# Attention one: the last pair's shift goes behind all scores, the scores are reordered, and the maximum's mask becomes one 128-row product a bank

## The reference

```python
def _L0_attn_ref(x, Wqkv, bqkv, Wr, br):
    xh = x.reshape(b, c, h, he).transpose(0, 2, 1, 3)
    qkv = jnp.einsum('bhce,ef->bhcf', xh, Wqkv) + bqkv
    q, k, v = jnp.split(qkv, 3, axis=-1)
    att = jnp.einsum('bhqe,bhke->bhqk', q, k) / jnp.sqrt(jnp.float32(he))
    mask = jnp.tril(jnp.ones((c, c), dtype=att.dtype), k=-1)
    att = jax.nn.softmax(att * mask, axis=-1)
    out = jnp.einsum('bhqk,bhke->bhqe', att, v)
    return out.transpose(0, 2, 1, 3).reshape(b, c, d) @ Wr + br
...
h = h + _L0_attn_ref(_layernorm(h, axis=-1), ...)
```

## Time and profile before

| what | us |
|---|---|
| median of 3 runs | 3225.5 (3218.67 to 3233.48) |
| the profiled execution | 3221.99 |
| its span, first to last instruction | 3220.2 |
| PE busy in the span | 2746.9 (85%) |
| DVE busy in the span | 2115.3 (66%) |
| POOL busy in the span | 1727.9 (54%) |
| ACT busy in the span | 1592.7 (49%) |

### The profile page before, as it was taken

The page is one execution under the profiler, slowest core; times in us unless marked ns, Lnnn a source line. Parts: engine busy times, 40 slices in busy tenths (PEclk is TensorE's granted clock), DMA queues, the critical chain, the costliest instruction groups (busy, mean ns, idle before and its releaser), DMA issues. The chain is left out here.

```text
span 3220.2 us, 61044 instructions
## 1 busy us (share of the span) xinstructions
PE 2746.9 (85%) x15254; PEld 1578.1 (49%) x15318; DVE 2115.3 (66%) x5668; ACT 1592.7 (49%) x3630; POOL 1727.9 (54%) x3076
## 2 busy tenths in 40 slices
PE   1678888888888888888887699989898979999999
PEld 1223433333333443334334466666666656666666
DVE  2545655665656656656563799989898976565554
ACT  1345555555545555455553265555555545444444
POOL 3663443334333343334433487777777757767766
PEclk7678888888878888888887799999999989999999
DMA  3352324333342323423243000000000000000000
GB/s 52 84 107 44 53 43 59 56 49 46 50 62 47 51 46 52 66 43 52 43 59 128 1 1 1 1 1 1 1 1 1 1 1 10 15 16 15 15 15 19
DMA packets 81303, 113.30 MB, mean 35 GB/s; under 512 B 25100, under 2 KB 37144, under 8 KB 80536
## 3 DMA queue, kind: packets, MB, share of 16 engines
q1 hardware_dynamic: 76360, 101.44, 19.5%
q0 software_dynamic: 3072, 8.39, 0.9%
q10 hardware_dynamic: 1744, 2.16, 0.2%
HBM read 18.98 MB, written 8.39 MB: 8 GB/s over the span
## 5 line engine op out<-in xcount | busy, mean ns | idle before, releaser
L495 ACT ACTIVATE probs<-scoresT 128x512 f32<-128x512 f32 (+3 forms) x1536 | 693.1, 490 | 610.2 <-PE scoresT L638 580.5
L587 DVE TENSOR_REDUCE cand<-ring 128x4 f32<-128x512 f32 x1152 | 720.4, 683 | 261.2 <-PE ring L688 197.6
L415 POOL TENSOR_SCALAR_AFFINE_SELECT probs<-probs 128x128 f32<-128x128 f32 x1024 | 294.3, 293 | 619.3 <-ACT probs L495 608.9
L638 PE MATMUL scoresT<-stage 98*128 98x512 bf16 (+3 forms) x1536 | 506.7, 386 | 70.4 <-ACT probs L495 61.8
L652 PE MATMUL pv<-probs,Vg 128*32 128x512 f32 (+3 forms) x3072 | 352.9, 569 | 5.0 <-POOL probs L415 5.0
L688 PE MATMUL ring<-Km,Qm 64*128 64x512 bf16 (+2 forms) x1792 | 251.4, 320 | 80.8 <-DVE cand L587 41.5
L638 PEld LDWEIGHTS scoresT<-stage 98*128 98x128 bf16 x1536 | 131.2, 100 | 375.3 <-ACT probs L495 241.4
L1115 PE MATMUL mm<-w_W,hT 128*128 128x256 f32 x1024 | 258.5, 398 | 9.1 <-ACT z L1203 3.5
L1135 PE MATMUL mm<-w_W,x2T 128*128 128x512 f32 x512 | 242.2, 596 | 0.3 <-DVE x L1354 0.2
L688 PEld LDWEIGHTS ring<-Km,Qm 64*128 64x128 bf16 x1792 | 83.8, 95 | 323.7 <-DVE cand L587 145.1
L1196 ACT ACTIVATE hT<-mmT,w_be,w_g 128x128 f32<-128x128 f32 x512 | 185.9, 469 | 90.2 <-PE mmT L1126 90.2
(11 more groups left out here) (254 smaller groups left out, 5367.5 us busy)
## 6 DMA issues: line engine op xcount, KB each, us to landing
stage<-parts SPq DMA_DIRECT2D x256, 96.0 KB
stage<-parts SPq DMA_DIRECT2D x256, 64.0 KB
Qm<-parts SPq DMA_DIRECT2D x128, 128.0 KB
Km<-parts SPq DMA_DIRECT2D x128, 128.0 KB
stage<-parts SPq DMA_DIRECT2D x256, 32.0 KB
out<-result SPq DMA_DIRECT2D x64, 128.0 KB, 1.7
stage<-ct SPq DMA_DIRECT2D x128, 4.0 KB
w_W<-in_W SPq DMA_DIRECT2D x4, 512.0 KB
```

The lines of the kernel that those rows point to most:

```text
L415: nc.gpsimd.affine_select(out=d, in_=d, compare_op=ALU.is_gt, fill=0.0, base=0, pattern=[[1, P]], channel_multiplier=-1).then_inc(mask_ok, 1)
L495: nc.scalar.activation(probs[:, n % 8, lo:hi], scoresT[u % SCORE_BANKS][:, lo % 512:(hi - 1) % 512 + 1], ACT.Exp, scale=SOFT).then_inc(exp ...
L587: ins = nc.vector.tensor_reduce(c, src[:].rearrange("p (t a b) -> p t a b", t=c.shape[1], b=P), AX.X, ALU.max)
L638: nc.tensor.matmul(scoresT[u % SCORE_BANKS][:, lo % 512:(hi - 1) % 512 + 1], Ks[0:ROWS, gi, hh, P * kt:P * kt + P], Qs[0:ROWS, gi, hh, lo: ...
```

## The change

Six things change, all in attention one.

1. Scores are taken in a new order: positions 2 to 5 hold (1, 0), (1, 1), (0, 2), (0, 3) instead of (0, 2), (0, 3), (1, 0), (1, 1). Pair 1's operands are first read at position 4 instead of 2.
2. The last `CT` (pair 1) and `EQ` move from position 28 or 29 to 31, behind every score and `PV`. `CT` waits for POOL's second instruction (`cm_c`) instead of its third (`cm_ok`).
3. `LOAD_MAX` follows `MAX_FINAL` directly, for both pairs, and waits until PE has filled the pair's last bank instead of for m.
4. `LOAD` waits for 4 x HPG = 16 units of the running group instead of 8.
5. The mask is two products over all 128 rows (one a bank) instead of four of 64 rows; the eight transfers that set up `ident2` and `future2` go.
6. In `AT` the maxima start at position 4 instead of 6 (gi 0) and 2 instead of 3 (gi 1), and end at 28 instead of 29 (gi 0).

```diff
+ORDER = [(kt, hh) for kt in range(TPB) for hh in range(HPG)]
+ORDER[2:6] = [(1, 0), (1, 1), (0, 2), (0, 3)]
...
 def score_units(kt, hh):
+    n = ORDER.index((kt, hh))
     if kt < TPB // 2:
-        u = 2 * (HPG * kt + hh)
-        return [(u, P * kt, 512), (u + 1, 512, S)]
-    return [(TPB * HPG + HPG * (kt - TPB // 2) + hh, P * kt, S)]
+        return [(2 * n, P * kt, 512), (2 * n + 1, 512, S)]
+    return [(TPB // 2 * HPG + n, P * kt, S)]
...
-    0: {... "MX": 6, "MX_END": 29, "MX_CURVE": 1.2},
-    1: {... "MX": 3, "MX_END": 28, "MX_CURVE": 1.2},
+    0: {... "MX": 4, "MX_END": 28, "MX_CURVE": 1.1},
+    1: {... "MX": 2, "MX_END": 28, "MX_CURVE": 1.1},
...
-                if p and k == 3:
+                if p and k == 4:
                     uses[-1] += [("R", "CT", "dve", p - 1)]
-                if p and k == 4 and load_max:
-                    uses[-1] += [("LOAD_MAX", p - 1)]
-            uses[-1] += [("MAX_FINAL", p)]
-        uses.append([("R", "CT", "dve", PAIRS_MX - 1), ("EQ",)] + ([("LOAD_MAX", PAIRS_MX - 1)] if load_max else []))
+            uses[-1] += [("MAX_FINAL", p)] + ([("LOAD_MAX", p)] if load_max else [])
...
+        at(31, ("R", "CT", "dve", PAIRS_MX - 1), ("EQ",))
...
-            kt, h = divmod(pos, HPG)
+            kt, h = ORDER[pos]
...
-                                wait_apart(sp, (parts_ok, 4 * (hb + 1 + e[0])), (st_ok, UNITS * (g - 1) + 2 * HPG))
+                                wait_apart(sp, (parts_ok, 4 * (hb + 1 + e[0])), (st_ok, UNITS * (g - 1) + 4 * HPG))
...
-                                wait_apart(sp, (parts_ok, 4 * (hb + 2)), (m_ok, PAIRS_MX * g + p + 1))
+                                wait_apart(sp, (parts_ok, 4 * (hb + 2)), (filled, num(last[-1][0], 0) + 1))
...
-                                for i in range(2):
-                                    for j in range(2):
-                                        ins = nc.tensor.matmul(out[j][:, P * at:P * (at + n)], ident2[half[j], i, :],
-                                                               future2[half[j], i:i + 1, :].broadcast_to([HALF, n, P]),
-                                                               start=start and i == 0, stop=stop and i == 1,
-                                                               tile_position=(half[j].start, 0))
+                                for j in range(2):
+                                    ins = nc.tensor.matmul(out[j][:, P * at:P * (at + n)], ident_b[:],
+                                                           future[:, None, :].broadcast_to([P, n, P]), start=start, stop=stop)
...
-                                pe.wait_ge(cm_ok, PAIRS_MX * g + e[4] + 1)
+                                pe.wait_ge(cm_c, 2 * (PAIRS_MX * g + e[4]) + 2)
```

More of the change, by code:

```diff
@@ L53, with masks_before @@
 SCORE_BANKS, RING_BANKS = 2, 4
+ORDER = [(kt, hh) for kt in range(TPB) for hh in range(HPG)]
+ORDER[2:6] = [(1, 0), (1, 1), (0, 2), (0, 3)]
 def score_units(kt, hh):
+    n = ORDER.index((kt, hh))
     if kt < TPB // 2:
-        u = 2 * (HPG * kt + hh)
-        return [(u, P * kt, 512), (u + 1, 512, S)]
-    return [(TPB * HPG + HPG * (kt - TPB // 2) + hh, P * kt, S)]
+        return [(2 * n, P * kt, 512), (2 * n + 1, 512, S)]
+    return [(TPB // 2 * HPG + n, P * kt, S)]
+def masks_before(kt):
+    return 1 + max(ORDER.index((kt, hh)) for hh in range(HPG))
 STAGE = 2 * HPG * S
@@ L84 @@
 AT = {
-    0: {"LN_STATS": 1, "LN_NORM": 3, "XT": 6, "PV_COPY": 0, "TMP": 0, "PT": 5, "OT": 21, "WR": 22, "RSUM": 5, "SUF": 9, "QK": 8, "QK_STEP": 2, "MID_LAG": 2, "V": 12, "VG": 0, "LOAD": 11, "MX": 6, "MX_END": 29, "MX_CURVE": 1.2},
-    1: {"PV_COPY": 0, "TMP": 0, "PT": 2, "WR": 1, "V": 8, "VG": 6, "LOAD": 6, "MX": 3, "MX_END": 28, "MX_CURVE": 1.2},
+    0: {"LN_STATS": 1, "LN_NORM": 3, "XT": 6, "PV_COPY": 0, "TMP": 0, "PT": 5, "OT": 21, "WR": 22, "RSUM": 5, "SUF": 9, "QK": 8, "QK_STEP": 2, "MID_LAG": 2, "V": 12, "VG": 0, "LOAD": 11, "MX": 4, "MX_END": 28, "MX_CURVE": 1.1},
+    1: {"PV_COPY": 0, "TMP": 0, "PT": 2, "WR": 1, "V": 8, "VG": 6, "LOAD": 6, "MX": 2, "MX_END": 28, "MX_CURVE": 1.1},
     "V_IN": 0, "WR_IN": 1,
@@ L255, in attention_one @@
         tmp_ok, rd_ok, o_ok = sem("tmp_ok"), sem("rd_ok"), sem("o_ok")
-        WEIGHTS = 8 * 2 + 2 + 8
+        WEIGHTS = 8 * 2 + 2
         def wait(eng, s, value):
@@ L327, in run @@
                             if section == "loop":
-                                wait_apart(sp, (parts_ok, 4 * (hb + 1 + e[0])), (st_ok, UNITS * (g - 1) + 2 * HPG))
+                                wait_apart(sp, (parts_ok, 4 * (hb + 1 + e[0])), (st_ok, UNITS * (g - 1) + 4 * HPG))
                             else:
                                 sp.wait_ge(parts_ok, 4 * (hb + 1 + e[0]))
-                                wait(sp, st_ok, UNITS * (g - 1) + 2 * HPG)
+                                wait(sp, st_ok, UNITS * (g - 1) + 4 * HPG)
                             for hh in range(HPG):
@@ L349, in run @@
                             else:
-                                wait_apart(sp, (parts_ok, 4 * (hb + 2)), (m_ok, PAIRS_MX * g + p + 1))
+                                last = [x for x in plans[section] if x[0] == e[0] and x[1:3] == ("R", "MX")
+                                        and x[4:6] == (2 * p + 1, MAX_BANKS - 1)][0]
+                                wait_apart(sp, (parts_ok, 4 * (hb + 2)), (filled, num(last[-1][0], 0) + 1))
                             lo = 16 * (HPG * (par if first else 1 - par) + 2 * p)
@@ L670, in mask @@
                             def mask(at, n, start, stop):
-                                for i in range(2):
-                                    for j in range(2):
-                                        ins = nc.tensor.matmul(out[j][:, P * at:P * (at + n)], ident2[half[j], i, :],
-                                                               future2[half[j], i:i + 1, :].broadcast_to([HALF, n, P]),
-                                                               start=start and i == 0, stop=stop and i == 1,
-                                                               tile_position=(half[j].start, 0))
-                                        if stop and i == 1 and at + n == 4:
-                                            ins.then_inc(filled, 1)
+                                for j in range(2):
+                                    ins = nc.tensor.matmul(out[j][:, P * at:P * (at + n)], ident_b[:],
+                                                           future[:, None, :].broadcast_to([P, n, P]), start=start, stop=stop)
+                                    if stop and at + n == 4:
+                                        ins.then_inc(filled, 1)
                             if every:
```

7 lines of the change are left out of this document (1 added, 6 removed).

## The result

| | us |
|---|---|
| changed kernel, median of 4 runs | 3281.2 (3274.98 to 3289.7) |
| kernel before, median of 4 runs beside it | 3227.9 (3218.67 to 3233.48) |
| ratio | 1.017 (95% interval 1.0136 to 1.0204) |
| ratio of a second measurement, on another chip | 1.0187 (1.0172 to 1.0203) |
| profiled execution, its span | 3274.98, 3273.2 |

The changed kernel is 1.7% slower, 53 us from one profiled execution (3221.99) to the other. The head of the changed kernel's page: PE's busy time fell by 62 us while the span rose by 53.

A forecast was written before the change was run, and what follows sets the result against it. Bound by PE's work plus waits shared by PE, ACT and DVE. Terms -70 + 165 - 9 + 14 - 15 = +85 us on 3222.0 gave 3307, with the median 3.5 higher: 3310 us; range 3232 to 3372.

The forecast's parts named there:

- LOAD's threshold, "one for one": Group gi 0: later `LOAD` lengthens ACT's wait before `QK` equally, 11.1 us, +165 us in all; gi 1 costs nothing.
- CT and EQ: Group end: moved behind the scores, PE's and ACT's stop for POOL's cf goes, -70 us (-60 to -75).
- The clock's term: Behind the `CT` stop: PE stays busy, so up to 1.9 us a half returns from half clock, -15 us (-28 to 0).
- PT's hold: Start of gi 0: `PT` waits for a DVE reduction, PE held 3.6 us, position 7 ends 2.8 us later.
- the pair of banks: Gi 0: one more pair of maxima banks done before the stop, 0.6 us in each of 15, -9 us (-20 to 0).
- The mask: 128-row mask between 64-row products: no columns saved, height changes of 0.09 us added, +14 us (0 to +23).
- bare weight loads: Mask: two uncovered loads of 0.095 us in each of 320 masks, +61 instead of +14; not adopted.
- The setup transfers: Before attention: the eight removed transfers end under DVE's wait for gathered rows, so they save nothing.
- the shift's cover: Next group's start: pair 1's shift lands some 4 us in, its reader at about 6, hidden with 2 us to spare.
- The length of a half: Two groups of attention one: expected to take 107 to 110 us instead of 102.4.
- The other signs: ACT waits 12 to 17 us, `LOAD` starts 15 to 18 us into gi 0, cf waits vanish, `PT` waits for `cand`.

The follow-up runs named there:

- order and `CT` alone: Kernel before with the new score order, last `CT`, `EQ` and `LOAD_MAX` 1 at position 31, `LOAD` at 10 units: ratio 0.9697, 3129 us.
- the split: Changed kernel with `LOAD` in two steps, pair 0's transfers waiting for 1 unit, pair 1's for 10: ratio 0.9537, 3076 us; with the old mask 0.9531.
- the split on order and `CT` alone: Kernel before with new score order, last `CT`, `EQ` and `LOAD_MAX` 1 at position 31, `LOAD` waiting for 1 unit (pair 0) and 10 (pair 1): ratio 0.9674.

## Why the prediction was right, and where its sum was off

The side and the mechanism were right: 3281 us, within 3232 to 3372; the forecast was 3310, +85 us where +53 came. By its own steps:

- **LOAD's threshold, "one for one": right in the changed kernel, a little too strong in the one before.** `LOAD` was to start 11.1 us later and did start 9.8 later (15.7 for 5.9); its time to ACT's release stayed 17.4 us; ACT's wait was to be 14 to 15 us and is 14.2. The two kernels that change only this number show it from both sides: +3.0% on the kernel before, -4.1% on the changed one. In the changed kernel 8.9 us of delay are 8.8 us of a half; in the kernel before 8.4 us are 6.8, and part of the difference came back in the other group, which the step denied.
- **CT and EQ: right, and too small with its clock.** The stops are gone. The prediction gave -70 for them and -15 for the clock; order and `CT` alone, with `LOAD` 1.3 us later than before, measure -99. If those 1.3 us count one for one in 15 halves, the term is about -119, an estimate from these two numbers, and this is the largest error, about the size of the whole miss of 32 us. The clock's term was priced from the end of gi 1 alone (4.05 against 2.16 us); the half-clock stretch at the start of gi 1, with `WR` at 3.38 instead of 1.99 us, was in the same listing and wasn't counted.
- **PT's hold: the mechanism right, the worth wrong.** It delays `LOAD` by 2.4 us where 2.8 was given. But the pair of banks ahead of the stop was priced at -9 us for all halves, 0.6 us each. Moving the maxima back changes nothing at 16 units, where it also takes the hold away, and costs 22 us at 10. The term should have been 1.4 us a half by the second, and 2.4 by the first if hold and banks cancel.
- **The mask: right about the 0.1 us of a change of height; its weight isn't confirmed.** +14 was given; no effect was measured with `LOAD` at 16 units or split, and 9 us, not clear of noise, at 10. The +61 us of bare weight loads are excluded by the split, by `LOAD` at 10 units and by the steps of 0.21 and 0.22 us.
- **The setup transfers and the shift's cover: as said.** The shift of pair 1 is issued around the next group's first score, and no wait for it appears.
- **The length of a half: missed.** 107 to 110 us were given as a sign, 105.8 came. The other signs (ACT's wait, the start of `LOAD`, the waits for cf, `PT` behind `cand`) came as said.

One chain of kernels adds up to the result, each step taken from the ratios above: -98 us for order and `CT` with `LOAD` at 10 units, +20 for the rest of the change at that threshold, +133 for 16 units instead of 10, together +55.

A further limit of such a sum: the length of a half moved in steps. Once a kernel had settled, it was 102.40 us in the kernel before, 105.81 in the changed one and with the old mask, 109.23 in the kernel before with 16 units, and 95.6 in the kernel with order and `CT` alone, with the split and without. Within each of these kernels the settled halves stay within 0.1 us of that value, and kernels that differ in their work have the same average to some 0.01 us, at a different mean clock (0.87 and 0.85 at 105.81). The first three lie 3.4 us apart, and 95.6 is twice that below the first. Not every kernel settles so: with `LOAD` at 10 units, with the maxima at 6 and with the split on the changed kernel, two to four different lengths follow each other in turn. So the result, +3.4 us a half, is a single step: the forecast found the side by a right mechanism, but a difference between two such values can't be shared out among small terms, and a small term may read zero where the half keeps its value. That may be why the mask at 16 units and the split on order and `CT` alone show next to nothing. The worth of such a term must be measured elsewhere. What makes the steps wasn't tried.

## What to carry to other kernels

When a semaphore threshold is raised to make a reordering safe, look up who waits for the work behind it, in another engine's queue: here eight more score units on SP were 8 us a half more of standing still on ACT. Ask for the smallest count that is still safe, and split the issue by what each part really waits for: 10 units instead of 16 made the same change 2.4% faster than before instead of 1.7% slower, and the split 4.6%. When a stop is removed, price the slow-clock stretches on both sides of it too.

## What was not expected of the hardware

- The average time of a half is the same to some 0.01 us in kernels with different work (105.81 with either mask; 95.6 with and without the split), while the mean granted clock can differ (0.87 and 0.85).
- Two stops of 4.4 us together cost 6.8 us a half, and the half had 34 us at 1.2 GHz with them and 17 without. In a single trace, the kernel before with 16 units, halves of the same work took 110.2 us at 0.81 and 105.0 at 0.89.
- The issue of 24 small transfers from one queue took 15.25 to 15.6 us in nearly all settled halves of every kernel, whatever the other engines did, so an engine's queue of transfers is a resource to be scheduled like the engines. Early in attention one it took up to 16.4 us in the kernel before.
